# Four of the eight transfers of rotated keys issued by ScalarE's queue instead of SyncE's, in the second layer of a two-layer decoder

## The reference

```python
def _L1_attn_ref(x, Wqkv, Wout):
    N_HEADS = 16
    BLOCK_SIZE = 64
    ...
    qkv = (x @ Wqkv.T).reshape(B, L, 3, H, HD).transpose(2, 0, 3, 1, 4)
    q, k, v = (qkv[0], qkv[1], qkv[2])
    q, k = (_rope(q), _rope(k))
    qb = q.reshape(B, H, nb, BS, HD)
    kb = k.reshape(B, H, nb, BS, HD)
    vb = v.reshape(B, H, nb, BS, HD)
    att = jnp.einsum('bhnqd,bhnkd->bhnqk', qb, kb) * scale
    causal = jnp.tril(jnp.ones((BS, BS), dtype=bool))
    att = jnp.where(causal, att, jnp.finfo(att.dtype).min)
    att = jax.nn.softmax(att, axis=-1)
    out = jnp.einsum('bhnqk,bhnkd->bhnqd', att, vb)
    out = out.transpose(0, 2, 1, 3).reshape(B, L, D)
    return out @ Wout.T
```

## Time and profile before

| what | value |
|---|---|
| runs | 3047.73, 3041.04, 3049.35 us; median 3047.73 |
| profiled execution | 3043.07 us; its span, first to last instruction, 3041.3 us |
| PE busy | 2707.5 us (89%) |
| PEld busy | 1579.5 us (52%) |
| DVE busy | 1508.0 us (50%) |
| ACT busy | 1149.9 us (38%) |
| POOL busy | 681.7 us (22%) |
| mean granted clock of PE | 0.936 of full speed |
| transfers of line 580 | 64, of 64 KB each |

### The profile page before, as it was taken

How to read it: one execution, slowest core, us unless ns; L and a number is a source line. 1 busy time by engine, 2 the same in 40 slices (tenths; PEclk the granted TensorE clock), 3 DMA queues, 4 the chain that set the end, 5 groups by cost and what they waited for, 6 DMA issues and landing times. The chain is left out here.

```text
span 3041.3 us, 40614 instructions
## 1 busy us (share of the span) xinstructions
PE 2707.5 (89%) x16481; PEld 1579.5 (52%) x16481; DVE 1508.0 (50%) x2382; ACT 1149.9 (38%) x1989; POOL 681.7 (22%) x364
## 2 busy tenths in 40 slices
PE   7779999999999999999869888988988998699997
PEld 4355534753285426653358653452542533487776
DVE  5565356833784277634611146346455554644442
ACT  4673245533472255424313225345344344011111
POOL 0254035801572065503320200000000000022222
PEclk9889999999999999999879879999899898699999
DMA  5540003100120003000179610100100101144443
GB/s 191 217 157 22 1 0 113 38 1 1 49 101 2 1 1 129 22 1 0 41 269 333 247 25 7 22 22 1 22 22 1 22 8 52 50 146 149 146 166 84
DMA packets 62130, 218.76 MB, mean 72 GB/s; under 512 B 12293, under 2 KB 28122, under 8 KB 45178
## 3 DMA queue, kind: packets, MB, share of 16 engines
q1 hardware_dynamic: 45802, 187.39, 17.1%
q0 software_dynamic: 9568, 18.75, 2.5%
q10 hardware_dynamic: 6576, 10.05, 0.9%
HBM read 171.98 MB, written 39.99 MB: 70 GB/s over the span
## 5 line engine op out<-in xcount | busy, mean ns | idle before, releaser
L610 PE MATMUL psum<-arena 128*128 128x256 f32 (+7 forms) x4160 | 1084.1, 412 | 67.7 <-ACT arena L1488 11.5
L610 PEld LDWEIGHTS psum<-arena 128*128 128x128 f32 (+1 forms) x4160 | 679.6, 200 | 423.9 <-issue 312.4
L2500 POOL TENSOR_TENSOR arena<-arena 128x1024 f32<-128x1024 f32 x128 | 299.9, 2370 | 110.2 <-DVE arena L1958 95.2
L1958 DVE TENSOR_TENSOR_SCAN arena<-arena,psum 128x512 f32<-128x512 f32 x256 | 291.5, 1201 | 26.1 <-PE psum L751 17.7
L751 PEld LDWEIGHTS psum<-arena 128*128 128x128 f32 x2048 | 242.9, 198 | 47.5 <-ACT arena L1518 40.3
L751 PE MATMUL psum<-arena 128*128 128x128 f32 x2048 | 253.5, 283 | 1.9 <-issue 1.9
L2535 POOL DMA_INDIRECT arena<-xn,arena x32 | 31.6, 987 | 959.8 <-DVE arena L2442 908.4
L2507 POOL TENSOR_TENSOR arena<-arena 128x1024 f32<-128x1024 f32 x32 | 75.9, 2373 | 656.8 <-ACT arena L1606 656.8
L2272 DVE TENSOR_REDUCE arena<-psum 128x1 f32<-128x512 f32 x256 | 163.0, 685 | 84.5 <-PE psum L1208 84.3
L2052 DVE SCALAR_TENSOR_TENSOR arena<-psum,arena 128x1024 f32<-128x1024 f32 x128 | 156.9, 1244 | 80.4 <-PE psum L896 80.1
L1606 ACT ACTIVATE arena<-arena 128x1024 f32<-128x1024 f32 x128 | 146.7, 1146 | 110.1 <-DVE arena L2052 109.9
(11 more groups left out here) (299 smaller groups left out, 3217.4 us busy)
## 6 DMA issues: line engine op xcount, KB each, us to landing
arena<-in_W SPq DMA_DIRECT2D x46, 1024.0 KB
arena<-c_rows SPq DMA_DIRECT2D x32, 512.0 KB, 3.8
arena<-in_Wg SPq DMA_DIRECT2D x16, 1024.0 KB, 4.9
arena<-in_Wu SPq DMA_DIRECT2D x16, 1024.0 KB, 7.6
arena<-in_Wd SPq DMA_DIRECT2D x16, 1024.0 KB, 10.0
arena<-in_xT SPq DMA_DIRECT2D x8, 512.0 KB, 5.4
zs_all<-arena SPq DMA_DIRECT2D x4, 1024.0 KB, 3.9
ut_all<-arena SPq DMA_DIRECT2D x4, 1024.0 KB, 8.7
```

Source lines behind the costliest of these rows:

```text
L610: r = mm(dst, w, x, start=i == 0, stop=i == len(pairs) - 1)
L1958: V.tensor_tensor_scan(hs[n % 3][:, c, :], dA[n % 2][:, c, :], bank[4 + c], 0.0, ALU.mult, ALU.add)\
L2500: nc.gpsimd.tensor_tensor(h, h, c_all[:, n % CBUFS, :].unsqueeze(1).broadcast_to([P, 2, L]), ALU.mult)\
```

## The change

Four of the eight transfers that spread the rotated keys (heads 4 to 7) are issued by ACT, and the other twelve of a round by SP. The transfer itself is put into a function that both call. ACT's part stands at the top of its round, ahead of the drains of the value tiles, behind a wait for the fourth `rope_step`. PE's wait for 256 of `qk_here` stays as it is.

```diff
+        def spread_head(eng, dst, src, h):
+            eng.dma_start(dst.rearrange("p (m g) n -> p m g n", g=2)[32 * (h % 4):32 * (h % 4) + LE, :, h // 4, :],
+                          src[LE * h:LE * (h + 1)]).then_inc(qk_here.sem, 16)
...
@@ SP
             for b in range(B):
                 for x, (dst, src) in enumerate(((rqT, rq), (rkT, rk))):
                     sp.wait_ge(rope_step.sem, rope_step.at(2 * x + 2, b))
-                    for h in range(8):
-                        sp.dma_start(dst.rearrange("p (m g) n -> p m g n", g=2)[32 * (h % 4):32 * (h % 4) + LE, :, h // 4, :],
-                                     src[LE * h:LE * (h + 1)]).then_inc(qk_here.sem, 16)
+                    for h in range(8 - 4 * x):
+                        spread_head(sp, dst, src, h)
                 if b >= 1:
                     store_out(b - 1)
...
@@ ACT
                 f = b - 1
+                w(rope_step, 4)
+                for h in range(4, 8):
+                    spread_head(act, rkT, rk, h)
                 v2c = v2.rearrange("p (c n) d -> p c n d", n=2)
                 for i in range(2):
                     t = LBA.take(act, 0, f"v2_{b}", i).rearrange("p (c n) -> p c n", c=2)
```

## The result

The changed kernel takes 3061.04 us, the median of 7 runs (3055.93 to 3067.62), beside 3048.12 us for the kernel before (7 runs, 3041.04 to 3049.82). The ratio is 1.0045 with a 95% interval of 1.0031 to 1.0059: 0.45% slower, some 14 us. Forecast were 3064.7 us with a range of 3051 to 3076. The profiled execution took 3062.21 us, its span 3060.1 us against 3041.3.

The account below looks back on a forecast made before the run. Prediction: PE is fullest, and one chain without slack (ACT's drains, PE's two tiles, scores, DVE) bounds the place. Drains 9.0 plus clock 8.0 made 17.0 us on the median 3047.73: 3064.7 us, range 3051 to 3076.

Parts of the forecast that it names:

- PE isn't waiting for the transfers: Before the block scores: transfers land just in time, so sooner landing is worth nothing, at most 0.5 us a round.
- ACT's wait costs nothing: Top of ACT's round: the wait for the fourth rotation ends 0.32 us before ACT could drain anyway; cost zero.
- The four issues delay the drains by 2.26 us: Ahead of ACT's value drains: four issues take 2.54 us at SP's price; four rounds cost 9.0 us.
- All of it passes down the chain: From drains through PE's two tiles and scores to DVE: no slack, so the whole 2.26 us reaches the scores.
- The clock falls in each round, 2.0 us each: PE's 3.1 us stop before the two tiles outlasts five earlier stops over 2 us, each with a fall; 8.0 us.
- Rival 1: At the two tiles the clock holds, leaving only the drains' delay: +9.0 us, 3056.8 us; chance 25%.
- Rival 2: ACT's queue takes the issues beside its compute, so drains aren't held: 3045.6 to 3047.7 us, taken 3046.7; chance 9%.
- Rival 3: SP's and ACT's queues obstruct each other, ACT free only after 5.18 us: 4.9 us a round, 3075.3 us; chance 6%.
- (1) to (3): Drains 2.6 us after the rotation; PE stops 3.1 us, no DMA named before scores; DVE idle over 10.3 us.
- (4): Granted clock is 0.50 for some microseconds within PE's two tiles, in most rounds.
- (5): From round 0's first value drain to the loop's end: 9 to 20 us longer, nothing else changing but clock falls.
- The sign of being wrong that is left: Low-clock spells elsewhere in the loop get shorter by as much as the new spells in the two tiles add.

Follow-up runs that it names:

- e7_yk_first: Kernel before with line 1089's two tiles ahead of the two value tiles on PE, lane and ACT; SP issues all transfers: ratio 0.9994 (0.9985 to 1.0003).
- e3_act_eight: Changed kernel, but ACT issues all eight key transfers ahead of the drains, SP only the queries: ratio to the kernel before 1.0075 (1.0062 to 1.0088).
- e5_after_filled: Changed kernel, but PE computes two unread extra tiles in its stop before line 1089's first tile: ratio to the kernel before 1.0034 (1.0021 to 1.0047).
- e6_act_behind: Changed kernel, but ACT's four issues stand behind all eight drains of the values: ratio to the kernel before 1.0002 (0.9993 to 1.0011).
- e9_act_middle: Changed kernel, but ACT's four issues stand behind the first four drains of the values: ratio to the kernel before 1.0000 (0.9988 to 1.0011).

## Why the prediction was right, point by point

- **PE isn't waiting for the transfers.** Right: with four issues by GpSimd and the last transfer landing sooner, DVE's idle time stays at 8.07 us. It was as near a tie as the prediction said, 0.25 us by e7_yk_first.
- **ACT's wait costs nothing.** Right to 0.06 us a round.
- **The four issues delay the drains by 2.26 us** (bounds 1.7 and 3.0). Measured 2.54 to 2.56: ACT takes 2.79 us for four where SP's 2.54 was taken. Nearly all of the 0.25 us is the one longer issue of a round, which is there only when ACT and SP start together; ACT alone has 0.64 us from one to the next (e3_act_eight). And there is 0.05 us from the last issue to the drain. The term is 10.2 us instead of 9.0.
- **All of it passes down the chain.** Right: 2.54 us in the drains, in PE's stop and in DVE's idle time of round 1.
- **The clock falls in each round, 2.0 us each.** The mechanism was right, the size was not: it fell in three rounds of four and cost 2.3, 0, 1.0 and 1.2 us, 4.5 in all instead of 8.0. The step that failed is the one from the five stops of more than 2 us, each with a fall, to a fall in each round. Two issues make stops of 2.1 us with no fall in four rounds, four make stops of 3.4 us with three falls, eight make stops of 5.8 us with four. So a stop as long as those five isn't enough here, and a longer one isn't sure to do it: rounds 1 to 3 of the changed kernel have the same stop between the same tiles, and the clock held in one and fell at different moments in the other two. What decides is open. In four of the five stops PE came from small matmuls (eight of 128x128, line 1112, behind 64 of 16x64), but the last came behind a dense tile of line 610 (four of 128x512, from 2559.95 us), so that isn't shown to be the difference. The second error is the price of a short spell. The prediction has 1.7 us for 3.4 us of it, taking half, and takes off PE's wait of 0.38 us between the tiles only for the long one. By the tiles' own times (3.48 and 1.96 us) a microsecond at the lower clock loses 0.44, so 3.4 × 0.44 - 0.38 = 1.1 us, and 1.0 and 1.2 were measured. The long spell of round 0 cost 2.3 us, within the 2.7 that the prediction has for a longer one.
- **The sum.** 10.2 + 4.5 = 14.7 us by the places, 13.7 by the ratio, against 17.0. The one term came out 1.2 us larger and the other 3.5 us smaller, so part of the nearness of 3061.04 to 3064.7 is two errors of opposite sign. The falls are counted in one execution; the runs of the changed kernel differ by 12 us among themselves.
- **Rival 1** (the clock holds, 3056.8 us) is what round 1 did, and e5_after_filled in all rounds. **Rival 2** (the drains aren't held) is wrong as put, since drains behind the issues are held; but its mechanism exists for compute that stands ahead, and e6_act_behind shows it. The Trainium skill's rule that was cited against it ("TensorE: Matmul & The Clock Gate", "Architectural detail: the array is 16× 32×32, not 1× 128×128": ACT's queue is strictly first in, first out) doesn't cover this: in e6_act_behind an issue at 1971.40 starts before four drains that stand ahead of it. Whether it holds among compute alone no run here tests. **Rival 3** (the queues obstruct each other, eight issues from two queues taking as long as eight from one) happened only in small: SP's four and ACT's four ran in 2.49 and 2.79 us side by side and not in 5.18. It did happen in the landing, which nobody waited for.
- **What the profile after would show.** (1) to (3) came as written: 2.88 us, a stop of 3.4 us, no DMA named, over 10.3 us of idle time in every round. "12 where the clock fell" is 11.7 and 11.8 in two rounds. (4) held in three rounds. (5) holds with 15.5 us. The sign of being wrong that is left didn't show: from the last rotated key of round 0 to the end of the loop the lower clock adds up to 119 us before and 130 after (the granted clock in windows of 5 us), of which about 14 are the three new spells, so the others got shorter by about 3 us, not by as much.

## What to carry to other kernels

Before a transfer is moved to a second queue, look at what stands behind it in the new issuer's program and who waits for that: the price is the issues' time, 0.65 to 0.70 us each for these, as a delay of the next compute, and whether it is paid depends on a few places in the program, not on the engine. Put behind compute that has just been handed over, the issues cost 0.2 us a round or nothing here. And test first whether the transfers are waited for at all: a row that names a DMA before a gap that is as long elsewhere without one need not be a wait, and turning the order of the work around it shows how near it is to being one.

## What the runs showed of the hardware

ACT's program runs ahead of ACT's compute: a DMA issue that stands behind four activations already handed over starts under them, and the activations go on beside it at 0.59 us each (e6_act_behind, e9_act_middle). With eight ahead of it the issue starts under the fourth, 1.83 us after the first.

Two engines that begin to issue at the same moment cost one of them about a quarter of a microsecond, once: ACT's second issue took 0.85 us in rounds 1 to 3 of the changed kernel, and 0.61 where ACT issued alone (e3_act_eight) or began 0.3 us after SP (e9_act_middle). The very first such issue of ACT, in round 0, took 0.74 us in all of them. What delays them isn't shown.

Small transfers from two queues at once move more bytes but land later each. In the kernel before, the DMA engines moved 101 GB/s while SP issued the keys of round 0:

```profile
1776.00:1780.00 4.00, 2.85 (x6) 1.16 (x7) 0.00 (x0) 3.68 (x7) 0.00 (x0) 1.00 0.62 101
```

Two windows of 1 us in round 0 of the changed kernel, where SP issues from 1777.56 to 1780.05 and ACT from 1777.57 to 1780.36 (GB/s last, the clock third from the right):

```profile
1779.00:1780.00 1.00, 0.54 (x3) 0.14 (x1) 0.00 (x0) 0.00 (x0) 0.00 (x0) 1.00 0.89 180
...
1782.00:1783.00 1.00, 0.04 (x1) 0.07 (x1) 0.00 (x0) 0.96 (x3) 0.00 (x0) 0.54 0.31 29
```

180 GB/s at the peak, where the same windows of the kernel before have at most 105. ACT's transfers take 4.0 us to land (median) and SP's beside them 3.6, where SP's eight alone took 2.4. With eight issued by ACT alone it was 2.4 us again, with ACT's issues spread among SP's last ones (e6_act_behind) 2.5. The second row has the fall of the clock: a mean of 0.54 in the microsecond at whose end PE resumed after its 3.41 us.
